# A pre-norm block with linear attention and a top-k router: output bias as one bf16 product, residual h added in PSUM, sums by accumulating DMA, a shorter ranking on two engines

## What is computed

```python
h = layernorm(x)                                  # eps 1e-5
q, k, v = h @ Wq + bq, h @ Wk + bk, h @ Wv + bv   # 16 heads of 8
q, k = elu(q) + 1, elu(k) + 1
k = k / sqrt(sum(k*k over the head) + 1e-6)
out = (q @ (k.T @ v) per head) @ Wo + bo          # linear attention, no softmax
y = h + out
x1 = x + layernorm(y, eps=1e-6) * gamma + beta
g = layernorm(x1)
scores = g @ w_router                             # one per token
top = the 768 of 1024 tokens of a batch with the highest scores
processed = gelu(g @ w_block)                     # tanh form
result = x1 + (processed where token in top, else g)
```

## Time and profile before

| | |
|---|---|
| Runs | 91.19, 91.26 and 93.52 us; median 91.26 |
| Profiled execution | 91.05 us, of which the span of instructions is 89.2 |
| Busy PE / PEld / DVE / ACT / POOL | 76.9 / 64.5 / 77.0 / 63.1 / 59.6 us |
| Mean granted clock of PE | 0.891 |
| Largest groups | L1315 and L1316 on PE, 12.6 and 12.4 us (64 products each); L657 on ACT 12.5; L467 on POOL 10.1; L1357 on PE 9.6 |

### The profile page before, as it was taken

The page is one execution under the profiler, slowest core; times in us unless marked ns, Lnnn a source line. Parts: engine busy times, 40 slices in busy tenths (PEclk is TensorE's granted clock), DMA queues, the critical chain, the costliest instruction groups (busy, mean ns, idle before and its releaser), DMA issues.

```text
span 89.2 us, 2508 instructions
## 1 busy us (share of the span) xinstructions
PE 76.9 (86%) x843; PEld 64.5 (72%) x843; DVE 77.0 (86%) x283; ACT 63.1 (71%) x213; POOL 59.6 (67%) x111
## 2 busy tenths in 40 slices
PE   4998589999999999999999999999999739877400
PEld 1345477766797999899899999989888639765300
DVE  4383999999999999999988698989868899999970
ACT  5012078999999996989981996778759999991000
POOL 5376686984995859779989898979979492000000
PEclk9999999999999999999999999999999655555555
DMA  0989789800099999991000000000000000033495
GB/s 26 297 234 269 276 289 382 314 4 0 7 112 134 145 134 145 128 139 19 0 0 0 7 0 0 0 0 4 7 4 0 7 0 0 7 118 125 155 372 182
DMA packets 8643, 9.02 MB, mean 101 GB/s; under 512 B 819, under 2 KB 6326, under 8 KB 8630
## 3 DMA queue, kind: packets, MB, share of 16 engines
q0 software_dynamic: 4160, 2.10, 21.6%
q1 hardware_dynamic: 4032, 6.49, 20.9%
q10 hardware_dynamic: 438, 0.26, 1.0%
HBM read 4.66 MB, written 2.10 MB: 76 GB/s over the span
## 4 chain that ended last, share of the span: by engine, by line
PE 60%; DVE 16%; DMA 6%; POOL 4%; issue 4%; SPq 2%; ACT 2%; DVEq 1%
PE bank L1338 8%; PE bank L1278 8%; PE bank L1315 7%; PE bank L1316 7%; PE bank L1272 7%; PE bank L1288 6%; DMA x_sb<-in_L_attn_x_dram 6%; PE bank L1357 5%; DVE x_sb L988 4%; PE bank L1240 4%; PE bank L1327 4%; DVE reach L934 3%; DVE rise L946 2%; PE bank L1366 2%; ACT norm_sb L609 1%
## 5 line engine op out<-in xcount | busy, mean ns | idle before, releaser
L1315 PE MATMUL bank<-M_sb,qT 128*128 128x128 f32 x64 | 12.6, 278 | 0.0
L657 ACT ACTIVATE norm_sb<-xb_sb,shift,gain 128x128 f32<-128x128 f32 x32 | 12.5, 501 | 0.0
L1316 PE MATMUL bank<-back,hT 128*128 128x128 f32 x64 | 12.4, 275 | 0.0
L609 ACT ACTIVATE norm_sb<-bank 128x128 f32<-128x128 f32 x32 | 8.4, 284 | 4.2 <-PE bank L1316 4.2
L467 POOL TENSOR_TENSOR x_sb<-x_sb,xb_sb 128x512 f32<-128x512 f32 x8 | 10.1, 1269 | 1.2 <-ACT x_sb L633 1.2
L1357 PE MATMUL bank<-ones,reach 128*16 128x1 bf16 x256 | 9.6, 164 | 1.4 <-DVE reach L934 1.2
L633 ACT ACTIVATE x_sb<-bank,r 128x128 f32<-128x128 f32 x32 | 9.6, 376 | 1.5 <-DVE s_col L909 1.5
L1338 PE MATMUL bank<-wz_c,hT 128*128 128x129 f32 x64 | 10.0, 286 | 0.0
L1315 PEld LDWEIGHTS bank<-M_sb,qT 128*128 128x128 f32 x64 | 9.7, 192 | 0.2
L1316 PEld LDWEIGHTS bank<-back,hT 128*128 128x128 f32 x64 | 9.7, 192 | 0.0
L1357 PEld LDWEIGHTS bank<-ones,reach 128*16 128x16 bf16 x256 | 7.5, 88 | 3.0 <-DVE reach L934 1.6
(11 more groups left out here) (149 smaller groups left out, 215.1 us busy)
## 6 DMA issues: line engine op xcount, KB each, us to landing
xb_sb<-in_L_attn_x_dram SPq DMA_DIRECT2D x4, 512.0 KB, 6.9
xb_sb<-beta_sb POOLq DMA_DIRECT2D x4, 512.0 KB, 8.2
x_sb<-in_L_attn_x_dram SPq DMA_DIRECT2D x7, 256.0 KB, 5.9
out_dram<-x_sb SPq DMA_DIRECT2D x7, 256.0 KB, 2.1
x_sb<-in_L_attn_x_dram SPq DMA_DIRECT2D x2, 128.0 KB, 2.7
out_dram<-x_sb SPq DMA_DIRECT2D x1, 128.0 KB, 2.2
out_dram<-x_sb ACTq DMA_DIRECT2D x1, 128.0 KB, 2.4
w_sb<-in_L_attn_Wq_dram ACTq DMA_DIRECT2D x1, 64.0 KB, 2.6
```

Of the source, the lines that this page charges most:

```text
L609: last = nc.scalar.activation(norm_sb[:, n], bank_of(("y", u))[:, t * P:(t + 1) * P], ACT.Square, accum_out=y_sq[:, n:n + 1])
L657: last = nc.scalar.activation(norm_sb[:, t], xb_sb[:, t], ACT.Identity, bias=shift3[:, t:t + 1], scale=gain3[:, t:t + 1])
L1315: nc.tensor.matmul(o, qT[:, u, t * P:(t + 1) * P], M_sb[:, b], start=True, stop=False)
L1316: last = nc.tensor.matmul(o, hT[:, u, t * P:(t + 1) * P], back[:], start=False, stop=True)
```

## The change

**Output bias and h.** `norm_sb` gets a 129th column for the ones (all 128 columns of h are now normalised; transposes take columns 1 to 128). `fold_back`, `copy_back` and the products with `back` are gone. `bo` is loaded to all partitions on ACT's queue, and a new function on DVE, `split_bo`, takes out its mean and splits it into three bf16 parts whose sum is the float32 value. They lie in rows 0, 32 and 64 of `bo_rows`, and one bf16 product with ones puts the bias into a bank of y. h itself is added to y in PSUM by DVE (`add_h`), ahead of the squares.

**x1.** For halves 0 to 5 (`Q` in `X1_BY`) DVE scales y by r2 and gamma into `exp_q` (`scale_y`), and POOL issues an accumulating DMA that adds it to `xb_sb` (`residual`, which before was DVE's for all halves). Halves 6 and 7 keep `y_gamma` and `residual` on DVE.

**GELU sums.** All eight `gelu_sum` become accumulating DMAs issued by POOL.

**Ranking.** Rises of sets 0 to 2 are made by ACT, those of set 3 by DVE. A rise is stored as plus or minus one (DVE: plus or minus a half) in rows of its own, and the step's size has moved into the weights (`rise_by`, filled by 16 small operations of ACT, `step_tables`), so that a move is one or two products instead of up to six: 40 instead of 96. `split_keys` is cut into `split_high` and `split_low` (one operation more per set); `low_keys` is one operation shorter, and `least` in `ties` is gone.

**Orders.** `norm_sum` is called by two tiles instead of four. The lists of calls of all engines and `BANK_USES` are rewritten; `rank_counts` moves up on POOL.

```diff
-    X1_BY = "DDDDDDDD"
+    X1_BY = "QQQQQQDD"
+    GELU_BY = "QQQQQQQQ"
+    RISE_BY = "AAAD"
...
@@ y_half (PE)
+                nc.tensor.matmul(tiles(y), ones16[:], bo_rows[:].unsqueeze(1).to_broadcast([P, TH, D]), start=True, stop=False)
                 for t in range(TH):
-                    o = y[:, t * P:(t + 1) * P]
-                    nc.tensor.matmul(o, qT[:, u, t * P:(t + 1) * P], M_sb[:, b], start=True, stop=False)
-                    last = nc.tensor.matmul(o, hT[:, u, t * P:(t + 1) * P], back[:], start=False, stop=True)
+                    last = nc.tensor.matmul(y[:, t * P:(t + 1) * P], qT[:, u, t * P:(t + 1) * P], M_sb[:, b], start=False,
+                                            stop=(t == TH - 1))
...
+            def split_bo():
+                dve.wait_ge(bo_in, 16)
+                link(nc.vector.tensor_reduce(bo_sum[:], bo_sb[:], AXIS.X, ALU.add))
+                link(nc.vector.tensor_scalar(bo_mean[:], bo_sum[:], 1.0 / D, None, ALU.mult))
+                link(nc.vector.tensor_scalar(bo_c[:], bo_sb[:], bo_mean[:, 0:1], None, ALU.subtract))
+                link(nc.vector.tensor_scalar(bo_high[:], bo_c[:], 0.0, None, ALU.add))
+                link(nc.vector.tensor_tensor(bo_rest[:], bo_c[:], bo_high[:], ALU.subtract))
...
+                nc.vector.tensor_scalar(bo_rows[0:1, :], bo_high[0:1, :], 0.0, None, ALU.add)
...
+            def add_h(u):
+                dve.wait_ge(y_full, u + 1)
+                y = tiles(bank_of(("y", u)))
+                nc.vector.tensor_tensor(y, y, norm_sb[:, TH * u:TH * u + TH, 0:D], ALU.add).then_inc(yh_done, 1)
...
@@ scale_y (DVE)
-                    last = nc.vector.scalar_tensor_tensor(out=norm_sb[:, n], in0=bank_of(("y", u))[:, t * P:(t + 1) * P],
+                    last = nc.vector.scalar_tensor_tensor(out=exp_q[:, u, t * P:(t + 1) * P], in0=bank_of(("y", u))[:, t * P:(t + 1) * P],
                                                           scalar=r2[:, n:n + 1], in1=gamma_sb[:], op0=ALU.mult, op1=ALU.mult)
...
@@ residual (POOL)
-                nc.gpsimd.tensor_tensor(xb_sb[:, a:a + TH], norm_sb[:, a:a + TH], xb_sb[:, a:a + TH],
-                                        ALU.add).then_inc(x1_pool_done, 1)
+                nc.gpsimd.dma_start(xb_sb[:, a:a + TH].rearrange("p t d -> p (t d)"),
+                                    exp_q[:, u], accum_op=ALU.add).then_inc(x1_summed[u], 16)
...
@@ rise_lanes (ACT, new)
+                nc.scalar.activation(rise[row:row + LANES, part, l].rearrange("p (b n) -> p b n", b=nb),
+                                     counts_of(s, i).unsqueeze(2).to_broadcast([LANES, nb, LANES]), ACT.Sign,
+                                     bias=0.5 - KEEP).then_inc(rise_done[s], 1)
...
@@ move_lanes (PE)
-                first = UPPER if i >= UPPER else 0
-                for j in range(first, i + 1):
-                    last = nc.tensor.matmul(lanes_of(s, i), rise_by[0:LANE_ROW + 1, :], rise[0:LANE_ROW + 1, j, l],
-                                            start=(j == first), stop=(j == i))
+                part, row = SLOTS[i]
+                k = RISE_KINDS.index(RISE_BY[s])
+                if part == 1:
+                    nc.tensor.matmul(lanes_of(s, i), rise_by[:, k, 0, :], rise[:, 0, l], start=True, stop=False)
+                last = nc.tensor.matmul(lanes_of(s, i), rise_by[0:row + 2 * LANES, k, part, :], rise[0:row + 2 * LANES, part, l],
+                                        start=(part != 1), stop=True)
...
```

More of the change, by code:

```diff
@@ L654, in norm_sum @@
+            def norm_sum(u, half):
                 act.wait_ge(shift3_done, group_of(SUM_GROUPS, u))
                 act.wait_ge(gain3_done, group_of(SUM_GROUPS, u))
-                for t in range(TH * u, TH * u + TH):
-                    last = nc.scalar.activation(norm_sb[:, t], xb_sb[:, t], ACT.Identity, bias=shift3[:, t:t + 1],
+                for t in range(TH * u + 2 * half, TH * u + 2 * half + 2):
+                    last = nc.scalar.activation(norm_sb[:, t, 0:D], xb_sb[:, t], ACT.Identity, bias=shift3[:, t:t + 1],
@@ L1014, in _ @@
             first_normalise(1)
+            split_bo()
             bn_x(2)
@@ L1031, in _ @@
+            k_half(3)
+            centre_wo()
+            key_sums(2)
+            k_half(4)
+            mask_vk(0)
+            key_sums(3)
             q_half(0)
-            key_norms(0)
-            k_half(3)
             q_half(1)
-            norm_keys(1)
-            key_sums(2)
-            key_sums(3)
-            k_half(4)
+            key_norms(1)
+            k_half(5)
+            add_h(0)
             q_half(2)
-            q_half(3)
-            centre_wo()
-            mask_vk(0)
@@ L1043, in _ @@
-            key_norms(1)
-            norm_keys(3)
-            k_half(5)
+            norm_keys(3)
+            add_h(1)
+            key_sums(4)
+            key_sums(5)
+            scale_y(0)
+            q_half(3)
+            key_norms(2)
+            mask_vk(1)
+            norm_keys(5)
+            k_half(6)
+            scale_y(1)
+            k_half(7)
+            add_h(2)
+            key_sums(6)
+            key_sums(7)
+            x1_stats(0)
             q_half(4)
-            key_sums(4)
@@ L1048, in _ @@
-            k_half(6)
-            key_sums(5)
+            mask_vk(2)
+            key_norms(3)
+            scale_y(2)
+            add_h(3)
             q_half(5)
-            y_gamma(0)
-            key_sums(6)
-            key_norms(2)
-            k_half(7)
-            mask_vk(1)
-            residual(0)
-            key_sums(7)
-            y_gamma(1)
-            x1_stats(0)
-            norm_keys(5)
-            residual(1)
+            add_h(4)
+            q_half(6)
+            norm_keys(7)
@@ L1082, in _ @@
-            residual(4)
-            x1_stats(4)
-            y_gamma(5)
-            rise_lanes(0, 0)
-            residual(5)
+            scale_y(3)
+            add_h(5)
+            scale_y(4)
+            score_cols(0, 1)
+            q_half(7)
+            score_cols(1, 0)
+            mask_vk(3)
+            x1_stats(2)
+            scale_y(5)
+            score_cols(1, 1)
+            split_high(0)
+            add_h(6)
+            reach_lanes(0, 0)
+            x1_stats(3)
+            add_h(7)
@@ L1104, in _ @@
-            rise_lanes(0, 2)
+            x1_stats(4)
+            reach_lanes(0, 1)
+            score_cols(3, 0)
+            score_cols(3, 1)
+            residual(6)
+            split_high(1)
+            reach_lanes(0, 2)
+            reach_lanes(1, 0)
+            score_cols(4, 0)
+            y_gamma(7)
+            x1_stats(5)
+            score_cols(4, 1)
+            reach_lanes(1, 1)
+            reach_lanes(0, 3)
+            x1_stats(6)
             residual(7)
@@ L1178, in _ @@
+            rise_lanes(3, 6)
             ties(2)
-            rise_lanes(3, 6)
-            merge(2)
             reach_lanes(3, 7)
@@ L1400, in _ @@
             k_proj(3)
-            fold_back()
             transpose_h(4)
```

715 lines of the change are left out of this document (373 added, 342 removed), and 20 rows, old and new, of the table BANK_USES.

## The result

The changed kernel took 97.52 us (median), against 91.44 for the kernel before: a ratio of 1.065, interval 1.056 to 1.075. One of the four runs of the kernel before, 93.52 us, was a slow one and is not in the ratio. The forecast was 88.8, with a range up to 91.8. The profiled execution took 97.44 us, its span 95.6 and its mean granted clock 0.873, where 0.891 stood before (the share of its full speed that PE was allowed, as the profile gives it).

A forecast was written before the change was run, and what follows sets the result against it. PE was taken as nearly full up to T, with DVE's 4.50 us of idle as the limit. T 67.4 + tail 16.6 + store 2.7 + 1.85 = 88.55, and 0.2 for the median: 88.8 us, range 86.0 to 91.8.

The forecast's parts named there:

- 3.0 of the 4.5 us close: In the first stretch, 3.0 of DVE's 4.5 us of idle vanish as PE has 4.7 us less work.
- T: End of the first stretch, at the last router score: 68.40 us before the change, forecast at 67.4.
- What is late next: If the way to x1, about 8.4 us, is not hidden: x1_stats(0) waits on DVE, q_half(4) and mask_vk(2) behind it.
- DVE's work before T: First stretch on DVE: split_bo +1.4, add_h +1.4, rises to ACT -1.4, key splits and reach +0.6; sum +2.0 us.
- ACT before T: ACT gains 10 rises and 16 table scalings at 0.17 us each, 4.4 us, into 10.8 us of idle.
- PE, POOL and the transfers: Output halves at 1.19 us each save PE 4.7 us; POOL issues take 1.0 us; 256 KB sums land in 4.
- The slow rival: Accumulating transfers land in 8.2 us like the beta adds, no idle closes, tail 19.5: 94.7 us; chance 0.12.
- The tail: From T to the last merge: ACT's list of rises, GELU and half sums takes 15.2 us; tail 16.6, not 18.1.
- the rival of the stalled rises: Behind T, ACT's rises wait for counts and hold half sums: tail 18 to 18.5, 90.3 to 91 us; chance 0.16.

The follow-up runs named there:

- The trade alone: Kernel before with the products with back gone and DVE adding h to y in PSUM, bias left out: 93.72 us, ratio 1.033.
- the mended form: Changed kernel with step tables early, rank_rows late, bo loaded behind x on SyncE's queue and split by ACT and POOL: 92.61 us, ratio 1.014.

## Why the prediction was wrong, step by step

**split_bo: wrong, the largest step.** The forecast gave it +1.4 us, 0 to 2.8, on the ground that the wait for x would cover half. The ten operations were sized well (9.16 to 11.77, 2.6 us against 2.8), and the wait for x did vanish behind them, all of its 1.37 us. What failed is a term that I put at nothing: the split waits for a transfer of its own, queued behind others, which landed at 9.1 us, and DVE idled 2.47 us for it. So 2.47 + 2.64 - 1.37 = 3.74, where +1.4 was forecast and 3.76 measured. Behind it stood the normalisation that PE's next half needs, and behind PE's wait the clock was down, at 0.50 from 15 to 20 us: the products at 16.08 and 17.95 took 2.08 and 1.92 us, where the same forms take 1.16 and 1.02 at a granted 1.00 (14.70 and 15.70 us with `bo` first), 1.8 us in all. The bias as a whole is worth 4.0 us in the changed kernel, the load and split alone 5.8 in the kernel before. I had costed the step's instructions and not its DMA.

**"3.0 of the 4.5 us close": wrong.** DVE's idle rose to 6.8 us, where the forecast left 1.5. With bias and tables out of the way (no bias, tables early, `rank_rows` late) it is still 60.85 - 56.02 = 4.8: the waits for PE's products did shrink (`s_col` from 1.2 to 0.3), but 1.2 us for the x1 transfer, 1.2 for POOL's root and 0.5 for ACT's exponential took their place. Taking one of these away did not help either: without the wait for the x1 transfer T came at 70.4 instead of 69.9. "What is late next" was named, `x1_stats(0)` on DVE, and then costed as hidden. The trade alone returns 1.5 us of idle for 4.2 us of DVE work, at a loss of 2.9 us. So the step that failed is that freed PE time comes back as DVE's waits fall: PE was not the only engine that DVE waits for.

**DVE's work before T: +5.2, not +2.0.** `add_h` less `y_gamma` (5.5 against 4.1 us, +1.4) and the rises that left (-1.5) came out as forecast. The rest is the split in full (2.4), keys and reaches (+1.0 against +0.6), two moments of x pushed into the stretch by the split (+0.7), the normalisations (+0.6) and one product of the keys that took 1.20 us instead of 0.68 (+0.5). The 128th column costs next to nothing: the median of the normalisations is 341 ns, against 338 before. Two of the twenty were long (1.03 and 0.85 us, at 17.35 and 17.61, beside POOL's fills of its tables), and so was the product of the keys at 24.58, beside POOL's own at 24.15. Shortest, median and longest of the normalisations (ns):

```profile
L905 DVE TENSOR_SCALAR norm_sb<-x_sb,bn,r x20: 329/341/1035, 13.1 to 27.8; 128x128 f32<-128x128 f32 x20
```

**ACT before T: one size and two places.** A step table's scaling takes 0.31 us, not 0.17; my row was 64 columns on one partition. And I set the sum against ACT's idle time instead of asking what stands behind each table: PE's `hk_sb`. `rank_rows`, moved ahead of the exponentials, had no term at all. Moving them back is worth 0.6 to 1.0 (tables, not clear of noise) and 0.9 (rows).

**PE, POOL and the transfers: the sizes were right.** A half of y is now one bias product, 0.21 us to the next start (0.30 was taken), and four products (eight in the trace) of 1.05 us together: 1.26, against 1.19 forecast. Yet PE's busy time before T did not fall: 57.81 us against 57.82. The low clock (the 1.8 us above) and the products of the start that moved behind 9.05 us took it up; where only the products with `back` went (h by DVE), it fell by 4.3 us, and in the mended form by 2.2. POOL's stretch was not lengthened by its issues (busy 48.17 us before T, 49.92 before the change). The slow rival's landings of 8.2 us did not come, with one exception: the first x1 sum, issued at 39.29 behind a `beta` add, is waited for until 46.54, 7.2 us. The trace shows 3.3 and 4.6 us to landing for 256 KB, on either side of the 4 that I took from half the bytes of the earlier trace rows.

**The tail: right, with more than one cause.** ACT's list behind T is as summed: 14 rises 2.1 us, GELU 2.4, half sums 11.2, together 14.55 us busy where 15.2 was taken, and the last half sum ends at 91.67, T + 15.8 as forecast. But I credited the shorter ranking and gave POOL's missing sums nothing in the tail. The GELU transfers alone give 16.47 us in the kernel before, with all rises still on DVE; the ranking alone gives 19.25, and 18 to 20 with rises on ACT. So the transfers suffice for the tail, and whether the rises on ACT add to it in the changed kernel was not tried.

**The rivals.** None of them is what happened. The slower case was there, at 94.7 us, by landings that did not happen. The one sentence that fits is the last: PE's clock could fall before T. I left it without a price, though PE's wait at 10 us was the place to ask for one. In the rival of the stalled rises a sum is off: 67.4 + 18 to 18.5 + 2.7 + 2.05 is 90.2 to 90.7, not 90.3 to 91.

What stays open: how the last 1.2 us of the mended form (92.61 against 91.46) divide between the trade, the ranking and the order of x1; by stage, in the profiled executions, T is 2.9 us later and the tail 1.3 shorter. Also open is what makes up the other 1.2 us of the ranking's loss (2.3 alone), beside the 1.1 of operations held up by POOL's sums, and when exactly PE's clock falls.
